# A second feed-forward that scatters gated expert rows onto the tokens' rows, in place of gathering them back

## The reference

```python
x = x + 0.5 * ffn(layernorm(x), wg, w1, b1, w2, b2)
x = x + attention(layernorm(x), Wq, bq, Wk, bk, Wv, bv, Wo, bo)
x = x + 0.5 * ffn(layernorm(x), wg, w1, b1, w2, b2)

# ffn: E = 8 experts, K = 2 a token, N = 4096, capacity = K * N // E = 1024
scores = softmax(xt @ wg); topv, topi = top_k(scores, 2)
topv = topv / sum(topv)
flat = one_hot(topi.T, E).reshape(K * N, E)        # all first choices, then all second ones
pos = sum((cumsum(flat, axis=0) - 1) * flat, -1)   # the token's place with its expert
valid = pos < capacity;  gate = topv * valid
disp[topi, pos] += xt * valid
y = relu(disp @ w1 + b1) @ w2 + b2                 # per expert: 128 -> 512 -> 128
out = sum over k of gate[k] * y[topi[k], pos[k]]
```

## Time and profile before

| | us |
|---|---|
| median of 3 runs | 598.71 (596.43 to 601.47) |
| the profiled execution | 599.48 |
| its span, first to last instruction | 597.2 |
| busy: PE, DVE, POOL, ACT | 356.8, 353.3, 258.2, 228.7 |
| POOL: 128 gathers L530, 128 gathers L728 | 127.4, 121.4 |
| granted PE clock, mean of the span | 0.813 |

### The profile page before, as it was taken

How to read it: one execution, slowest core, us unless ns; L and a number is a source line. 1 busy time by engine, 2 the same in 40 slices (tenths; PEclk the granted TensorE clock), 3 DMA queues, 4 the chain that set the end, 5 groups by cost and what they waited for, 6 DMA issues and landing times. The chain is left out here.

```text
span 597.2 us, 5848 instructions
## 1 busy us (share of the span) xinstructions
PE 356.8 (60%) x1713; PEld 283.0 (47%) x1713; DVE 353.3 (59%) x1032; ACT 228.7 (38%) x408; POOL 258.2 (43%) x292
## 2 busy tenths in 40 slices
PE   0682177999998043878678692268899997000000
PEld 0571155888886023645456590246788885000000
DVE  6449656878778153687763848646778775122221
ACT  1239033766764022343542232325766764000000
POOL 6000475566520572556510000176566520677773
PEclk9999997999999555798998655559999999555555
DMA  9910012233321210111100130012223222232322
GB/s 256 284 43 1 18 49 58 70 73 96 80 54 35 70 53 19 40 44 42 40 15 0 52 90 1 10 49 63 75 76 97 76 54 56 53 88 70 88 70 66
DMA packets 47856, 38.43 MB, mean 64 GB/s; under 512 B 5747, under 2 KB 42641, under 8 KB 47825
## 3 DMA queue, kind: packets, MB, share of 16 engines
q1 hardware_dynamic: 39168, 20.98, 12.5%
q0 software_dynamic: 8512, 17.08, 11.4%
q10 hardware_dynamic: 144, 0.00, 0.0%
HBM read 23.36 MB, written 14.68 MB: 64 GB/s over the span
## 5 line engine op out<-in xcount | busy, mean ns | idle before, releaser
L530 POOL DMA_INDIRECT xg<-xn_dram,gidx x128 | 127.4, 995 | 213.2 <-POOLq L1175 84.5
L728 POOL DMA_INDIRECT yg<-y_dram,slot x128 | 121.4, 949 | 88.8 <-issue 37.4
L610 ACT ACTIVATE hf<-psum,bcol 128x512 f32<-128x512 f32 x128 | 88.4, 692 | 77.3 <-PE psum L555 57.6
L645 DVE TENSOR_TENSOR hl<-hf,hh 128x512 fp32r<-128x512 f32 x128 | 88.0, 691 | 13.9 <-ACT hh L612 8.4
L553 PE MATMUL psum<-xh,wres 128*128 128x512 f32 x128 | 55.8, 436 | 5.1 <-DVE xl L634 5.1
L638 DVE CAST hh<-hf 128x512 fp32r<-128x512 f32 x96 | 42.0, 437 | 20.1 <-ACT hf L610 19.2
L564 PE MATMUL psum<-hh,wres 128*128 128x512 f32 x128 | 53.2, 415 | 0.0
L554 PE MATMUL psum<-xl,wres 128*128 128x512 f32 x128 | 52.4, 409 | 0.0
L555 PE MATMUL psum<-xh,wres 128*128 128x512 f32 x128 | 52.2, 408 | 0.0
L566 PE MATMUL psum<-hh,wres 128*128 128x512 f32 x128 | 50.6, 395 | 0.0
L565 PE MATMUL psum<-hl,wres 128*128 128x512 f32 x128 | 50.5, 394 | 0.0
(11 more groups left out here) (168 smaller groups left out, 676.7 us busy)
## 6 DMA issues: line engine op xcount, KB each, us to landing
y_dram<-y_sb SPq DMA_DIRECT2D x32, 256.0 KB
wexp_raw<-in_L_ffn_w SPq DMA_DIRECT2D x16, 256.0 KB, 6.0
xn_dram<-xns SPq DMA_DIRECT2D x16, 256.0 KB, 2.5
x_sb<-in_L_attn_x SPq DMA_DIRECT2D x8, 256.0 KB, 4.5
xg<-xn_dram,gidx POOLq DMA_INDIRECT x128
yg<-y_dram,slot POOLq DMA_INDIRECT x128
out<-last SPq DMA_DIRECT2D x8, 256.0 KB
wraw<-in_L_attn_Wq POOLq DMA_DIRECT2D x1, 64.0 KB, 3.6
```

The lines of the kernel that those rows point to most:

```text
L530: gp.indirect_dma_start(out=self.xg[:, s % 4, t], out_offset=None, in_=xn_dram, in_offset=bass.IndirectOffsetOnAxis(ap=gidx[:, j:j + 1], a ...
L610: one = nc.scalar.activation(self.hf[:, c], bank[1 + c][:], ACT.Relu, bias=bcol[:, at:at + 1])
L645: dve.tensor_tensor(self.hl[:, s % 2, c], self.hf[:, c], self.hh[:, s % 2, c].bitcast(F32), ALU.subtract).then_inc(hl_ready[c], 1)
L728: gp.indirect_dma_start(out=self.yg[:, n % YB, k, t], out_offset=None, in_=y_dram, in_offset=bass.IndirectOffsetOnAxis(ap=slot[:, k, GT * ...
```

## The change

Only the second feed-forward changes. Instead of storing results by slot and gathering them by token, each slot's row is scaled by its gate and added to the token's row in HBM by an indirect DMA with an add, issued by POOL. For this:

- `acc_dram`, 4096 rows and 128 spare ones, is filled with x at the start of the routing block (SP, 9 DMAs). Slots that hold no token add to the spare rows.
- the stored normalized rows become 130 wide (`xw_dram`): 128 channels and both gates of the token (`row_gates`), so the slot's gate comes with its row. The stores go out after the gates, the eight groups one after the other, from eight buffers.
- DVE derives for each slot its target row, and whether it holds a first or a second choice, from the expert's counts (`taken`, `slot_targets`), and picks the gate (`gates_of`).
- POOL's order in the experts block: gathers of chunks 0 to 4, then for each chunk s its four scatters and the four gathers of chunk s+5. Before the scatters of an even chunk it waits for those of the two chunks before to have landed, since an expert's two chunks never hold the same token but two experts may.
- the last block copies `acc_dram` to the output in two halves, issued by SP and ACT, after all scatters have landed. L728's gathers, L1219 and L1227 are gone, and so are the 16 stores L519 of this stage.

```diff
+XW = C + K
+XG = 8
+YG = 4
+AHEAD = 5
...
-                self.xns = new("xns", [P, XB, GT, C])
+                self.xb = XB if f == 0 else NG
+                self.xns = new("xns", [P, self.xb, GT, C if f == 0 else XW])
...
+            def sync_wide(self, sp):
+                for g in range(NG):
+                    sp.dma_start(rows(acc_dram, g * SEQ), x_sb[:, GT * g:GT * g + GT]).then_inc(acc_begun, 16)
+                sp.dma_start(acc_dram[N:N + P, :], x_sb[:, 0]).then_inc(acc_begun, 16)
+                sp.wait_ge(norm_dve, 2 * NG)
+                sp.wait_ge(norm_act, 2 * NG)
+                sp.wait_ge(xw_ready, 2)
+                for g in range(NG):
+                    sp.dma_start(rows(xw_dram, g * SEQ), self.xns[:, g]).then_inc(xw_stored, 16)
+                sp.wait_ge(xw_stored, 16 * NG)
+                sp.wait_ge(acc_begun, 16 * (NG + 1))
...
-                ch.add(dve.tensor_reduce(base[:], pos[:], AX, ALU.add))
+                if f == 0:
+                    ch.add(dve.tensor_reduce(base[:], pos[:], AX, ALU.add))
+                else:
+                    self.row_gates(dve, ch)
                 dve.wait_ge(counts_done, f + 1)
...
+                if f == 1:
+                    ch.then(dve.tensor_reduce(taken[:], bank[4].rearrange("p (e k t) -> p e k t", e=E, k=K), AX, ALU.add))
                 dve.wait_ge(inverse_done, f + 1)
...
+            def row_gates(self, dve, ch):
+                column = lambda k: self.xns[:, :, :, C + k]
+                by_row = lambda a: a.rearrange("p (g t) -> p g t", t=GT)
+                dve.wait_ge(exp_gap, self.f + 1)
+                ch.then(dve.tensor_scalar(total[:], e2[:], 1.0, None, ALU.add))
+                ch.then(dve.reciprocal(gap[:], total[:]))
+                dve.tensor_scalar(column(0), by_row(gap[:]), 0.5, None, ALU.mult).then_inc(xw_ready, 1)
+                dve.scalar_tensor_tensor(column(1), by_row(gap[:]), 0.5, by_row(e2[:]), ALU.mult, ALU.mult).then_inc(xw_ready, 1)
+
+            def slot_targets(dve, ch):
+                ch.then(dve.tensor_tensor(taken[:, :, 1], taken[:, :, 0], taken[:, :, 1], ALU.add))
+                ch.then(dve.tensor_scalar(taken[:], taken[:], -float(TOKEN0), None, ALU.add))
...
+                ch.add(dve.tensor_tensor(by_slot(first_choice), at_slot, taken[:, :, 0:1].to_broadcast([P, E, NCH]), ALU.is_lt))
+                ch.add(dve.tensor_tensor(by_slot(filled), at_slot, taken[:, :, 1:2].to_broadcast([P, E, NCH]), ALU.is_lt))
+                ch.then(dve.tensor_scalar(no_token[:], token_id[:, 0:1], -1.0, -float(TOKEN0 + N), ALU.mult, ALU.add))
+                ch.then(dve.tensor_scalar(targetf[:], gidx[:], no_token[:], None, ALU.add))
+                ch.then(dve.tensor_tensor(targetf[:], targetf[:], filled[:], ALU.mult))
+                dve.tensor_scalar(target[:], targetf[:], no_token[:], None, ALU.subtract).then_inc(targets_known, 1)
...
+            def gather_and_scatter(self, gp):
+                def gather(s):
+                    if s >= XG:
+                        gp.wait_ge(xT_ready, NSB + s - XG + 1)
+                        gp.wait_ge(slot_gates, s - XG + 1)
+                    for t in range(GT):
+                        j = GT * s + t
+                        gp.indirect_dma_start(out=self.xg[:, s % XG, t], out_offset=None, in_=xw_dram,
+                                              in_offset=bass.IndirectOffsetOnAxis(ap=gidx[:, j:j + 1], axis=0)).then_inc(slot_rows_in[s % XG], 16)
+
+                def scatter(s):
+                    if s == 0:
+                        gp.wait_ge(targets_known, 1)
+                    elif s % 2 == 0:
+                        for before in (s - 2, s - 1):
+                            gp.wait_ge(scattered[before % YG], 64 * (before // YG + 1))
+                    gp.wait_ge(y_ready, NSB + s + 1)
+                    for t in range(GT):
+                        j = GT * s + t
+                        gp.indirect_dma_start(out=acc_dram, out_offset=bass.IndirectOffsetOnAxis(ap=target[:, j:j + 1], axis=0),
+                                              in_=self.y_sb[:, s % YG, t], in_offset=None, compute_op=ALU.add).then_inc(scattered[s % YG], 16)
+
+                for s in range(AHEAD):
+                    gather(s)
+                for s in range(NSB):
+                    scatter(s)
+                    if s + AHEAD < NSB:
+                        gather(s + AHEAD)
...
+                def gates_of(s):
+                    one, other = (self.xg[:, s % XG, :, C + k] for k in range(K))
+                    ch.then(dve.tensor_tensor(self.dg[:, 0], one, other, ALU.subtract))
+                    ch.then(dve.tensor_tensor(self.dg[:, 1], self.dg[:, 0], first_choice[:, GT * s:GT * s + GT], ALU.mult))
+                    dve.tensor_tensor(self.gs[:, s % YG], self.dg[:, 1], other, ALU.add).then_inc(slot_gates, 1)
+
+                def gated_rows(s):
...
+                    for t in range(GT):
+                        last = dve.tensor_scalar(self.y_sb[:, s % YG, t], bank[6][:, t * P:(t + 1) * P], self.gs[:, s % YG, t:t + 1], None, ALU.mult)
+                    last.then_inc(y_ready, 1)
...
                 if b > 0:
-                    Route.slots_and_gates(dve, ch, self.f)
+                    Route.slot_targets(dve, ch)
+                    gates_of(0)
...
             def _(act):
                 route.scalar_norm(act)
+                route.scalar_gate(act)
                 route.scalar_rows(act, act_chain(act))
-                route.scalar_gate(act)
...
+        with nc.Block() as block:
+            halves = N // 2
+            def half(dram, h):
+                return dram[h * halves:(h + 1) * halves, :].rearrange("(p t) c -> p (t c)", p=P)
+            def copy_out(eng, h):
+                for u in range(YG):
+                    eng.wait_ge(scattered[u], 64 * NSB // YG)
+                eng.dma_start(half(of, h), half(acc_dram, h)).then_inc(out_stored[h], 16)
+                eng.wait_ge(out_stored[h], 16)
...
```

More of the change, by code:

```diff
@@ L673, in vector @@
                         low(s + 1)
+                        if b > 0:
+                            gates_of(s + 1)
                     if here:
@@ L1132, in _ @@
                 def _(sp):
-                    experts.sync(sp)
+                    if f == 0:
+                        experts.sync(sp)
                 @block.gpsimd
                 def _(gp):
-                    experts.gpsimd(gp)
+                    if f == 0:
+                        experts.gpsimd(gp)
+                    else:
+                        experts.gather_and_scatter(gp)
                 @block.tensor
@@ L1196, in macaron, with _ @@
         experts_block(1)
-        with ExitStack() as stage, nc.Block() as block:
-            gather = Gather(stage, 1)
-            last = scoped(stage, "last", [P, 2, GT, C])
-            @block.gpsimd
-            def _(gp):
-                gather.gpsimd(gp)
-            @block.vector
-            def _(dve):
-                for n in range(NG):
-                    u = n % 2
-                    for k in range(K):
-                        dve.wait_ge(yg_in[k][n % YB], 64 * ((NG + n) // YB + 1))
-                        if k == 1:
-                            dve.wait_ge(yg_used[0], NG + n + 1)
-                        elif n >= 2:
-                            dve.wait_ge(out_stored[u], 16 * (n // 2))
-                        for t in range(GT):
-                            at = GT * n + t
-                            one = dve.scalar_tensor_tensor(last[:, u, t], gather.yg[:, n % YB, k, t], gate[:, k, at:at + 1],
-                                                           x_sb[:, at] if k == 0 else last[:, u, t], ALU.mult, ALU.add)
-                        one.then_inc(yg_used[k], 1)
+        with nc.Block() as block:
[7 more added lines that the diff above has]
+                eng.wait_ge(out_stored[h], 16)
             @block.sync
             def _(sp):
-                for n in range(NG):
-                    sp.wait_ge(yg_used[1], NG + n + 1)
-                    sp.dma_start(rows(of, n * SEQ), last[:, n % 2]).then_inc(out_stored[n % 2], 16)
-                for u in range(2):
-                    sp.wait_ge(out_stored[u], 16 * NG // 2)
+                copy_out(sp, 0)
+            @block.scalar
+            def _(act):
+                copy_out(act, 1)
 _INS = ["L0_attn_x", "L0_attn_Wq", "L0_attn_bq", "L0_attn_Wk", "L0_attn_bk", "L0_attn_Wv", "L0_attn_bv", "L0_attn_Wo",
```

72 lines of the change are left out of this document (49 added, 23 removed).

## The result

The change made the kernel slower: 632.1 us against 597.6, a ratio of 1.057 (95% interval 1.050 to 1.065), where 578 was forecast and 608 was the upper end of the range. The profiled execution has a span of 630.5 us; the forecast's sum had its end at 576.1 on the same scale, 54.4 us too early.

The account below looks back on a forecast made before the run. PE and POOL were taken to take turns, POOL's 64 output gathers following the experts. Replacing everything from 509.5 to 597.2 moved the end to 576.1 (span -21.1); with 2.3 around it, 578 us, range 565 to 608.

Parts of the forecast that it names:

- step 3: Experts loop: POOL alternates four scatters and four gathers, 88 DMAs at 1.28 us each, 112.6 us, ending at 526.7.
- Rival (c): POOL's issue of an accumulating scatter is dearer, up to 1.39 us: +28 us, 606; chance 0.12.
- Step 1: Routing: accumulator and wide-row stores stay hidden, gates add 0.5 us to the path; first gather at 385.55.
- Rival (d): Wide rows' stores end after the indices, or the output copy is slow: 10 to 20 us back, 588 to 600; chance 0.06.
- Its mark, a first gather after 387: Routing's end: the first gather starting after 387 us was to show late wide-row stores.
- Step 2: First gathers: POOL issues 20 without a wait, then idles 3.4 us for the first chunk's rows, until 414.1.
- the cover: Experts loop: rows come with 5 us in hand; four gathers (5.1 us) lie before each even chunk's wait for landing.
- rival (a): Experts loop and tail: scatter landings replace POOL's idle time; gain cancelled at 7.4 us landing, 604 at 8; chance 0.09.
- (b): Scatter stage: DMA engines serve accumulated rows one after the other; 675 us at 3.5 us an engine per scatter; chance 0.08.
- rival (e): Experts stage: DVE's casts hold POOL off, 1.89 us a scatter instead of 0.95: +60 us, 638; chance 0.03.
- Step 4: Tail after the last gather: 20 scatters at 1.25 us, 25.1 us, and three landings of 4.1 us, ending at 564.1.
- Step 5: Copy to the output: 8 us of transfer and 4.0 fixed, 12 us, ending at 576.1.

Follow-up runs that it names:

- p1: The changed kernel with 32 more POOL DMAs in its last block, eight forms of four, each issued after the one before landed; ran once, 726.2 us.
- e1: The changed kernel with its 64 scatters issued without the add: 558.8 us, ratio 0.981 to the kernel before.
- r2: The changed kernel again, unedited, in the faster kind of session: 597.9 us against 571.1, ratio 1.047.
- p2: The changed kernel with POOL DMAs of 64, 32 or 16 rows added in its last block, four of each form; ran once, 701.1 us.
- e2: The changed kernel with each scatter replaced by a gather from the accumulator into a spare tile: 554.0 us, ratio 0.974 to the kernel before.
- e7: The changed kernel with its two output copies issued inside the experts block, without a barrier before them: 594.8 us, ratio 1.046 to the kernel before.
- e3: The changed kernel with 8 chunks gathered before the first scatter instead of 5: 598.7 us, ratio 1.049 to the kernel before.
- e5: The changed kernel with plain scatters into two planes, added on DVE, 5 chunks ahead: 615.5 us, ratio 1.032 to the kernel before; again, 565.6 us, 0.991.

## Why the prediction was wrong

**The step that failed is the price of a scatter in step 3.** It took 0.98 us of issue, by the gather's row, and bounded it by 1.39; it is 1.635 in the kernel and 1.556 alone (p1). Of the 54.4 us, 64 x (1.635 - 0.977) = 42 are this one term, 20 x 0.67 = 13 of it in the tail, and e1's POOL is busy 41.6 us less with its scatters than r2's when the add alone is taken out. The gathers made dearer by it are 4.5 more. The rest is 6.9 ahead of the first gather, 5.1 of first wait, and about 5 the other way from the landings and the end. The working had put the surplus of an add into the rows (a read more for each), and so bounded it by the rows' part of a gather's issue, 0.44. p2 shows that the surplus is nearly fixed, 0.46 us at 16 rows and 0.59 at 128, which the rows' part of a gather's issue could not bound. Rival (c) named the place and gave 606 with 0.12; it decided at +0.33 a scatter, as written, but the surplus was 0.65, above the 0.44 at which it stopped. The direct DMAs of the earlier trace rows, whose 0.05 us for 126 rows more I read as "the form is cheap", said only that rows are cheap; they said nothing of the add.

**Step 1, routing:** right. +0.1 us against +0.5, and the wide stores ended in time: the stretches from 376 to 380 and 384 us moved 189 and 197 GB/s at DMA shares of 1.27 and 1.25, the indices came at 391.1, and the first gather followed them 1.38 us later, against 1.36 before. Rival (d) did not come up; the 6.9 us by which the first gather was late came with the first half, ahead of the edited lines. Its mark, a first gather after 387, was met without the stores, so that mark did not tell what it was meant to.

**Step 2, the first wait:** 8.5 us instead of 3.4. In the trace ACT's copy of the third chunk stood in a wait that the trace puts down to no engine:

```profile
418.37 0.58 ACT L691 CAST xh<-psum 128x512 fp32r<-128x512 f32 x1 [5.03 <-remote]
```

p1 and p2, in slower sessions too, waited 11.8 and 11.0 us there; e1, e2, e7 and r2, in sessions without such waits, 1.1 to 1.9, under the forecast. That the remote waits are the reason is argued from this; nothing took them away alone.

**Step 3, the cover:** right. Before the even chunks of the loop no wait of POOL for a landing shows but one of 0.3 at most, so rival (a) is out. The DMA share stayed at 0.3, so (b) is out. PE's clock fell to 1.2 GHz for parts of each round and cost nothing in this kernel: POOL's waits for rows of results are 8.5 us, all before the first scatter. DVE's neighbourhood, rival (e), is worth at most 0.08 us a scatter: 1.635 with DVE and all else at work, 1.556 alone, though single ones took up to 2.09. The Trainium skill's rule on the shared port (SBUF — State Buffer, "SBUF: two separate sides") therefore describes at most those 0.08 us here; the scatters from 589 us on, where DVE is busy 2.3 of 27 us, still take 1.55 to 1.57.

**Step 4, landing:** 2.4 us, not 4.1. The next scatter starts 2.43 us after the last one's issue ends, of which 0.3 is the usual gap; p1 has 1.9 for an add against 1.5 for a plain scatter. The add costs 0.4 us of landing, where the sum had put a store's 2.5 on top of a gather's 1.6.

**Step 5, the end:** the copy takes 8.8 us from issue to the end of the span where 12 were forecast, the barrier that was counted as hidden takes 4.4 (e7), and the last landing 1.9 of the 4.1. That the whole end is off by only 1.0 is luck: three errors cancel.

Most of the gain that was forecast was there to be had: with gathers of 0.96 us in the scatters' place the program is 2.6% faster than before (e2), against 3.5%. It was spent on 0.6 us for each of 64 issues, on the one engine that had become the bound.

## What to carry to other kernels

Where a change makes the engine that issues DMAs the bound, the price of one issue is the whole forecast: a form that the trace does not show should get a range that reaches past its nearest relative by a multiple, or be measured alone, which four DMAs in a row do. An accumulating indirect DMA of 128 rows cost POOL 1.56 us against 0.97, and most of the surplus stayed at 16 rows, so here it would have paid only with idle time left on POOL after the move. A plain scatter into separate planes with the adds on DVE got 1.5% in faster sessions and lost 1.6 to 3.2% in slower ones, where long waits on ACT stretched a schedule that hangs on one queue. And a run that gains what was expected may gain it for another reason: e3's 6 us lay in shorter issues, not in the wait that it was to remove.

## What the hardware showed that was not expected

- An add costs POOL 0.46 us at 16 rows and 0.59 at 128 in an indirect DMA; 0.30 in a direct one of 128 rows, which at 512 rows issues in 1.27.
- The input's 64 gathers average 1.05 us beside adding scatters, 0.99 beside plain ones and 0.98 beside gathers.
- The barrier behind a block whose last work is POOL's indirect DMAs costs about 4.4 us past the landing (e7 against the changed kernel).
- The kernel before took 597 us in one session and 571 in another on one chip, and e5's kernel 615 and 566; the trace of e5's slower session has the waits called remote, that of the faster has none.
- One stretch of attention ran at a granted clock of 0.53 in one run and 0.83 to 0.91 in four others, and attention took about 7 us longer in it.
